# A state-space scan on one Trainium2 core: convolutions in column halves, relu moved to VectorE, small steps moved off it

## The reference, cut to what matters

```python
x = einsum('bld,ed->bel', ctx, in_proj_w)            # 512 channels
x = silu(causal_conv(x, conv_w, 4 taps) + conv_b)    # = u
dt_low, Bm, Cm = split(einsum('bdl,ed->bel', x, x_proj_w))
dt = softplus(einsum('brl,dr->bdl', dt_low, dt_proj_w) + dt_proj_b)
A  = -exp(A_log)                                     # 16 states a channel
# for each position l, channel d and state n:
#   state = state * exp(dt*A) + dt*u*B ;  y[d] = sum_n state*C
y = (y + D*u) * silu(layernorm(input x))
```

## Time and profile before

| | us |
|---|---|
| three runs | 1542.57, 1548.24, 1553.94; median 1548.24 |
| the profiled execution | 1534.55 |
| its span in the profile | 1532.7 |
| first scan to last scan | 45.1 to 451.5 |
| VectorE, ScalarE, TensorE, GpSimd busy over the span | 1098.2, 995.3, 1423.5, 639.0 |

### The profile page before, as it was taken

The page is one execution under the profiler, slowest core; times in us unless marked ns, Lnnn a source line. Parts: engine busy times, 40 slices in busy tenths (PEclk is TensorE's granted clock), DMA queues, the critical chain, the costliest instruction groups (busy, mean ns, idle before and its releaser), DMA issues. The chain is left out here.

```text
span 1532.7 us, 20749 instructions
## 1 busy us (share of the span) xinstructions
PE 1423.5 (93%) x6056; PEld 611.8 (40%) x6057; DVE 1098.2 (72%) x1603; ACT 995.3 (65%) x1538; POOL 639.0 (42%) x422
## 2 busy tenths in 40 slices
PE   6688988978988999999999899799999999999999
PEld 2344444434444444444444344233333333244444
DVE  7999999999995522222222488899999999548985
ACT  4999999999974112333332244588878787868764
POOL 0579689688976431075757555200000000410000
PEclk7799999999998999999999999799999999999999
DMA  6212314113206349778943656433233233430464
GB/s 200 65 50 85 94 56 124 41 56 111 76 1 215 116 138 181 186 207 275 322 130 98 215 175 166 119 83 76 76 93 79 74 79 94 147 110 14 93 145 119
DMA packets 181210, 183.45 MB, mean 120 GB/s; under 512 B 104611, under 2 KB 132643, under 8 KB 180371
## 3 DMA queue, kind: packets, MB, share of 16 engines
q1 hardware_dynamic: 114422, 128.02, 29.0%
q10 hardware_dynamic: 57776, 24.89, 6.8%
q0 software_dynamic: 8944, 29.70, 6.4%
HBM read 96.97 MB, written 54.92 MB: 99 GB/s over the span
## 5 line engine op out<-in xcount | busy, mean ns | idle before, releaser
L275 POOL TENSOR_TENSOR m_hs<-m_hs,m_C 128x1024 f32<-128x1024 f32 x128 | 305.2, 2403 | 61.5 <-DVE m_hs L496 60.5
L1929 DVE TENSOR_REDUCE a_mx<-a_s 128x2 f32<-128x1024 f32 x256 | 303.3, 1218 | 32.7 <-PE a_s L2049 29.2
L496 DVE TENSOR_TENSOR_SCAN m_hs<-m_dA,m_d 128x512 f32<-128x512 f32 x256 | 294.8, 1201 | 12.3 <-PE m_d L650 11.1
L650 PE MATMUL m_d<-ident_sb,m_dBuT 128*128 128x128 f32 x1024 | 159.1, 288 | 25.1 <-DVE m_hs L496 16.7
L650 PEld LDWEIGHTS m_d<-ident_sb,m_dBuT 128*128 128x128 f32 x1024 | 116.4, 145 | 149.7 <-DVE m_hs L496 70.5
L383 ACT ACTIVATE m_dA<-m_dt,m_negA 128x512 f32<-128x512 f32 x256 | 167.8, 711 | 6.8 <-DMA m_dt<-m_dt 6.1
L1367 PE MATMUL e_gu<-e_w,e_xgT 128*128 x376 | 169.2, 593 | 0.0
L1762 POOL TENSOR_TENSOR x_sb<-x_sb,bo_sb 128x512 f32<-128x512 f32 x16 | 19.7, 1292 | 341.7 <-DVE a_m L1945 341.7
L2049 PE MATMUL a_s<-ring_sb 96*128 96x512 bf16 x512 | 151.1, 387 | 7.2 <-DVE a_mx L1929 5.1
L361 ACT ACTIVATE m_dBuT<-m_dtuT,m_BT 128x512 f32<-128x512 f32 x235 | 154.1, 711 | 0.4 <-PE m_d L650 0.3
L665 PE MATMUL m_y<-m_hs,m_fold 128*64 128x512 f32 x512 | 142.6, 637 | 0.5 <-POOL m_hs L275 0.5
(11 more groups left out here) (342 smaller groups left out, 2346.3 us busy)
## 6 DMA issues: line engine op xcount, KB each, us to landing
e_w<-in_ex_gu SPq DMA_DIRECT2D x16, 1024.0 KB, 7.3
ring_sb<-qk_dram SPq DMA_DIRECT2D x64, 192.0 KB, 3.1
xg_dram<-zeros_sb SPq DMA_DIRECT2D x47, 256.0 KB, 3.1
yg_dram<-attn_sb ACTq DMA_DIRECT2D x47, 256.0 KB, 3.8
m_C<-c_dram SPq DMA_DIRECT2D x64, 128.0 KB, 2.9
m_dt<-m_dt SPq DMA_DIRECT2D x64, 128.0 KB, 2.4
e_w<-in_ex_dn SPq DMA_DIRECT2D x16, 512.0 KB, 8.9
ring_sb<-qk_dram SPq DMA_DIRECT2D x64, 128.0 KB, 3.2
```

The lines of the kernel that those rows point to most:

```text
L275: pool.tensor_tensor(hs[:, J % RH], hs[:, J % RH], C2[:, N % RC].unsqueeze(1).broadcast_to([P, 2, L]), ALU.mult).then_inc(s_hc, 1)
L496: dve.tensor_tensor_scan(hs[:, J % RH, h], dA[:, j % RA], pd[j % RD][:], 0.0, ALU.mult, ALU.add)\
L650: last = pe.transpose(pd[j % RD][:, t * P:(t + 1) * P], dBuT[:, N % 2, t, g], ident[:])
L1929: dve.tensor_reduce(mx[:, r % 2, h * TB + 2 * c:h * TB + 2 * c + 2], psc[c][:], AX.X, ALU.max)\
```

## The change

1. `convolve`: each of the four steps is done in two halves of 256 columns. A half waits for its own half's step before, so there are two chains. 8 instructions a tile (`TAPS`), 128 in place of 64.
2. For the batches 1 to 3, the relu of dt leaves ScalarE's `logs` and becomes `relu` on VectorE: for tile 0 between the two scans of slot 12, for the others behind the scans of slots 14, 17 and 20 and ahead of `log1p` and L486. ScalarE waits for it before |z|.
3. Layer norm columns: EPS becomes the bias of ScalarE's root; the negated mean and its product with 1/std are made by GpSimd behind its products of slots 2 and 3 of batch 0.
4. Slot 127: GpSimd multiplies only the first half by C, VectorE the second, right behind the last scan. The order after it changes: VectorE gate sums 0 to 2, add 0, gate sum 3, adds 1 and 2, small steps, add 3; TensorE turns tiles 0 and 1, then takes the sums of slot 127, then turns tiles 2 and 3.

```diff
 # GpSimd
+                if J == LAST - 1:
+                    pool.wait_ge(s_scan, 2 * J + 1)
+                    pool.tensor_tensor(hs[:, J % RH, 0], hs[:, J % RH, 0], C2[:, N % RC], ALU.mult).then_inc(s_hc, 1)
+                    continue
...
+                if J == 2:
+                    pool.wait_ge(s_ln, LN_VAR)
+                    pool.tensor_scalar(nmr[:], mv[:, :, 0], -1.0, None, ALU.mult).then_inc(s_nm0, 1)
+                if J == 3:
+                    pool.wait_ge(s_ln, LN_RSTD)
+                    pool.wait_ge(s_nm0, 1)
+                    pool.tensor_tensor(nmr[:], nmr[:], rstd[:], ALU.mult).then_inc(s_nm, 1)
 # ScalarE, gates
-                    act.wait_ge(s_ln, LN_READY)
+                    act.wait_ge(s_nm, 1)
 # ScalarE, logs
                 if p >= 1:
-                    act.wait_ge(s_d2[et], 64 * p)
-                    act.wait_ge(s_dtu, m - E4 + 1)
+                    act.wait_ge(s_rel, m + 1)
                 z = bank(p, et)
                 act.activation(ee[:, et % 2], z[:], ACT.Abs, bias=dt_b[:, et:et + 1]).then_inc(s_abs, 1)
-                act.activation(dt[:, et], z[:], ACT.Relu, bias=dt_b[:, et:et + 1]).then_inc(s_rel, 1)
+                if p == 0:
+                    act.activation(dt[:, et], z[:], ACT.Relu, bias=dt_b[:, et:et + 1]).then_inc(s_rel, 1)
 # ScalarE, slot 3 of batch 0
-                        act.activation(rstd[:], rstd[:], ACT.Sqrt).then_inc(s_sd, 1)
+                        act.wait_ge(s_eps, 1)
+                        act.activation(rstd[:], mv[:, :, 1], ACT.Sqrt, bias=lead[:, 2, 0:1]).then_inc(s_sd, 1)
 # VectorE, convolve
-                dve.tensor_scalar(conv[:, et], z[:], conv_w[:, et, 3:4], None, ALU.mult).then_inc(s_cv, 1)
+                for lo in (0, L // 2):
+                    dve.tensor_scalar(conv[:, et, lo:lo + L // 2], z[:, lo:lo + L // 2], conv_w[:, et, 3:4], None,
+                                      ALU.mult).then_inc(s_cv, 1)
                 for k in range(1, 4):
-                    dve.wait_ge(s_cv, 4 * m + k)
-                    dve.scalar_tensor_tensor(conv[:, et, k:L], z[:, 0:L - k], conv_w[:, et, 3 - k:4 - k],
-                                             conv[:, et, k:L], ALU.mult, ALU.add).then_inc(s_cv, 1)
+                    for i, lo, hi in ((0, k, L // 2), (1, L // 2, L)):
+                        dve.wait_ge(s_cv, TAPS * m + 2 * k - 1 + i)
+                        dve.scalar_tensor_tensor(conv[:, et, lo:hi], z[:, lo - k:hi - k], conv_w[:, et, 3 - k:4 - k],
+                                                 conv[:, et, lo:hi], ALU.mult, ALU.add).then_inc(s_cv, 1)
+
+            def relu(p, et):
+                m = E4 * p + et
+                dve.wait_ge(s_dtp, m + 1)
+                dve.wait_ge(s_d2[et], 64 * p)
+                dve.wait_ge(s_dtu, m - E4 + 1)
+                dve.tensor_scalar(dt[:, et], bank(p, et)[:], dt_b[:, et:et + 1], 0.0, ALU.add, ALU.max).then_inc(s_rel, 1)
 # VectorE, layer norm: L524 (+EPS) and L530 (negated mean times 1/std) removed
 # VectorE, loop over slots
                 scan(J, 0)
+                if p < B and s == 12:
+                    relu(p, 0)
                 scan(J, 1)
+                if J == LAST - 1:
+                    N = J // E4
+                    dve.wait_ge(s_c[N % RC], 32 * (N // RC + 1))
+                    dve.wait_ge(s_scan, 2 * LAST)
+                    dve.tensor_tensor(hs[:, J % RH, 1], hs[:, J % RH, 1], C2[:, N % RC], ALU.mult).then_inc(s_hl, 1)
...
+                if p < B and s in (14, 17, 20):
+                    relu(p, (s - 11) // 3)
                 if p < B and s in (13, 15, 18, 21):
                     log1p(p, (s - 12) // 3)
```

More of the change, by code:

```diff
@@ L28 @@
 EPS = 1e-5
-LN_VAR = 2 * NT + 1
-LN_RSTD = 2 * NT + 2
-LN_READY = 2 * NT + 3
+LN_VAR = 2 * NT
+LN_RSTD = 2 * NT + 1
 def mamba(nc, x_sb, ident, identb, tg, a, c_dram, xg_dram, zeros, s_zero, lead):
@@ L43, in mamba @@
     AHEAD = RA // 2 - 1
+    TAPS = 8
     EARLY = NT - 2
@@ L110, in mamba @@
         s_sd = sem("ln_std")
+        s_nm0 = sem("ln_mean_negated")
+        s_nm = sem("ln_columns_ready")
         s_negA0 = sem("expA")
@@ L138, in mamba @@
         s_hc = sem("output_terms")
+        s_hl = sem("last_output_terms")
         s_y = sem("summed")
@@ L292, in silu @@
                 for et in parts:
-                    act.wait_ge(s_cv, 4 * (E4 * p + et + 1))
+                    act.wait_ge(s_cv, TAPS * (E4 * p + et + 1))
                     if p >= 1:
@@ L522, in variances_last @@
                     dve.bn_aggr(mv[:, t], stats[:, t]).then_inc(s_ln, 1)
-                dve.wait_ge(s_ln, 2 * NT)
-                dve.tensor_scalar(rstd[:], mv[:, :, 1], EPS, None, ALU.add).then_inc(s_ln, 1)
             def ln_columns():
@@ L528, in ln_columns @@
                 dve.reciprocal(rstd[:], rstd[:]).then_inc(s_ln, 1)
-                dve.wait_ge(s_ln, LN_RSTD)
-                dve.scalar_tensor_tensor(nmr[:], mv[:, :, 0], -1.0, rstd[:], ALU.mult, ALU.mult).then_inc(s_ln, 1)
             dve.wait_ge(s_wa, 16 * 5)
@@ L563, in _ @@
                 gate_sum(B - 1, et)
-            for et in range(E4 - 1):
-                add(B - 1, et)
+            add(B - 1, 0)
+            gate_sum(B - 1, E4 - 1)
+            add(B - 1, 1)
+            add(B - 1, 2)
             dve.wait_ge(s_lead, 2 * TB + 2)
@@ L569, in _ @@
             dve.tensor_tensor(lead[:, 0], lead[:, 0], lead[:, 1], ALU.mult).then_inc(s_lead, 1)
-            gate_sum(B - 1, E4 - 1)
             add(B - 1, E4 - 1)
@@ L582, in project @@
                 if p >= 1 and et >= 1:
-                    pe.wait_ge(s_cv, 4 * (E4 * p + et))
+                    pe.wait_ge(s_cv, TAPS * (E4 * p + et))
                 if p >= 3 and et == 0:
@@ L596, in project_u @@
                     if et == 0 and p >= 1:
-                        pe.wait_ge(s_cv, 4 * E4 * (p + 1))
+                        pe.wait_ge(s_cv, TAPS * E4 * (p + 1))
                     last = pe.matmul((py[0] if p == 0 else pm)[0:RX, :], w_xp[:, et], u[:, et], start=(et == 0),
@@ L613, in dt_product @@
                 if p == 0:
-                    pe.wait_ge(s_cv, 4 * (et + 1))
+                    pe.wait_ge(s_cv, TAPS * (et + 1))
                 elif et == 0:
@@ L663, in sums @@
                 pe.wait_ge(s_hc, J + 1)
+                if J == LAST - 1:
+                    pe.wait_ge(s_hl, 1)
                 for h in range(2):
@@ L723, in _ @@
             pe.wait_ge(s_scan, 2 * LAST)
-            for et in range(E4 - 1):
+            for et in range(2):
                 turn(B - 1, et)
             sums(LAST - 1)
-            turn(B - 1, E4 - 1)
+            for et in range(2, E4):
+                turn(B - 1, et)
 NE = 16
```

## The result

| | before | after |
|---|---|---|
| median of the runs, us | 1550.32 (6 runs, 1542.57 to 1556.23) | 1570.23 (6 runs, 1559.05 to 1577.48) |
| profiled execution, span | 1532.7 | 1568.4 |
| first scan to last scan | 405.2 | 430.9 |
| last scan's end to the stage's last add | 6.8 | 7.7 |
| the stage's last add ends at | 458.3 | 485.2 |

The ratio is 1.0138, with a 95% interval of 1.0099 to 1.0177: the change makes the kernel 21 us slower (15 to 27). Forecast was +12.3, in a range that holds the result. The scan stage alone is 26.9 us longer in these two profiles, and 22.7 us in a second pair (e10 and e11, 456.7 and 479.4). The other 8.9 us of the span lie in later stages, which the change doesn't touch and whose length varied from 1074 to 1094 us over the profiles of this study; nothing is concluded from them.

The account below looks back on a forecast made before the run. The prediction took VectorE's own instructions as the bound. Convolutions +3.0, layer norm -2.8, relus +11.3 and the end +0.8 gave +12.3 us, 1560.5 us from 1548.24, range 1541 to 1577.

Parts of the forecast that it names:

- rival 3: Convolutions: half steps don't overlap, each costs 0.52 us, 16 convolutions +18 us, total +27.7, 1576 us; chance 0.16.
- within 1%: Whole kernel: the time changes by no more than about 1% (15 us) either way; chance 0.75.
- three signs of being wrong: Scan stage: L486 stays at 0.46 us, TensorE's scan waits become long lower-clock pieces, or scans begin waiting for decays.
- Rival 2: Scan stage: ScalarE is the bound, relu and layer norm savings are gained, stalls aren't paid: 1538 us; chance 0.10.
- Convolutions: 16 convolutions on VectorE: eight half steps at 0.40 us, 3.20 against 3.01 us, +0.19 each, +3.0 us in all.
- Layer norm: Batch 0: VectorE without L524 gains 1.7 us, without L530 half of 2.2: together -2.8 us (-3.9 to -1.7).
- the gates still waiting about 1.4 us: Layer norm: ScalarE's gates get their columns from GpSimd at about the same moment as before, still waiting about 1.4 us.
- Relu, slot 12: Relu between two scans falls into their waits for TensorE: about +0.1 us a batch, no delay of ScalarE.
- Relu, slot 14: Relu puts L486 behind the start of GpSimd's product, so L486 waits for its end: +2.37 us a batch.
- Relu, slot 15: L475 now meets GpSimd's long product and takes 2.38 us instead of 1.14: +1.2 us a batch.
- Relu, slots 17 and 20: +0.66 us each, offset by VectorE's waits for the logarithm going away: about +0.1 us in sum a batch.
- The end: Slot 127: VectorE's half product waits for GpSimd's, its queue shifts 1.1 us, an idle 0.75 may go: +0.8 us.

Follow-up runs that it names:

- e10: The kernel before, profiled once more, unchanged: 403.8 us from first to last scan.
- e11: The changed kernel, profiled once more, unchanged: 425.2 us from first to last scan.
- e1: The changed kernel with the relus of batches 1 to 3 back on ScalarE: 402.7 us from first to last scan, ratio 1.0016 to the kernel before.
- e7: The kernel before with the layer norm part alone: 407.0 us from first to last scan, ratio 0.9987.
- e4: The changed kernel with TensorE's products to dt for tiles 2 and 3 one slot earlier: 417.1 us from first to last scan.
- e6: The changed kernel with L486 ahead of slot 14's relu and tiles 2 and 3's dt products one slot earlier: 410.6 us first to last scan, ratio 1.0043.
- e9: The changed kernel with every relu between a slot's two scans, tiles 1 to 3's logs and corrections one slot later: 411.1 us first to last scan, ratio 1.0022.
- e3: The changed kernel with L486 issued ahead of the relu in slot 14: 416.6 us from first to last scan.
- e5: The kernel before, relu left on ScalarE, with unused VectorE work of like length at the relu's four places: 419.1 us from first to last scan.
- e8: The kernel before with the halved convolutions alone: 412.1 us from first to last scan.

## Why the prediction was right, and which steps of it were not

The sign, the stalls of slots 14 and 15 and the end were forecast with their mechanism and their size. That the result lies in the range is in part luck: the forecast of +12.3 us had its own span of 1550 to 1570 us, at whose upper end the measured time lies, and the top of the wider range, 1577, was worked out for rival 3, which is out. The likeliest call, within 1%, was missed (1.4%). Batch 1, forecast to be 4 us longer, was longer by 10.4 and 7.2. Of the three signs of being wrong one came: TensorE's lower clock, which rose from 58 and 65 us up to the last scan in the two profiles of the kernel before to 82 and 75 in those of the changed one, though the scans' own waits for TensorE stayed at 9.4 us (9.7 before).

- **What bounds.** VectorE's instructions set the pace and ScalarE doesn't, though both were full: e1 puts the relus back on ScalarE and is faster. Rival 2 is out.
- **Convolutions.** Forecast 3.20 us each; the changed kernel shows 3.10, from 52.50 to 55.60, and 5.95 against 5.83 for a slot that holds one. Half steps last 0.47 to 0.48 us, where 0.50 was forecast, and follow each other at 0.39 us in the mean.
```profile
52.50 0.84 DVE L479 TENSOR_SCALAR m_conv<-m_misc,m_conv_w 128x256 f32<-128x256 f32 x2
53.26 2.42 DVE L484 SCALAR_TENSOR_TENSOR m_conv<-m_misc,m_conv_w,m_conv 128x255 f32<-128x255 f32 x6
55.60 2.32 DVE L521 TENSOR_TENSOR_SCAN m_hs<-m_dA,m_d 128x512 f32<-128x512 f32 x2
```
  So +0.12 and not +0.19 each, +1.9 us for 16. Rival 3 is out: by it a slot would have grown by 1.1 us and not 0.12. The Trainium skill's page "VectorE: DVE Perf Modes", section "The DRAIN you can't avoid", says that a semaphore after each instruction costs nothing extra; this case's trace differs, with 0.77 us from start to start with a wait and 0.67 without. No run has the half steps with a wait for the one just ahead, so what they would cost isn't shown.
- **Layer norm.** -2.8 was forecast. By slots 0 to 8 of batch 0, without what the halves add, the second pair of profiles shows -2.2, the first -0.7 and e7 -0.2. VectorE did get the 1.7 and the 2.2 us (slot 4 starts 3.7 us earlier). The step that failed is "the gates still waiting about 1.4 us": they no longer wait and start at 67.83 us, not at 69.38. But ScalarE got no more than these 1.5 us, and in slot 7 VectorE stands before ScalarE's inputs: TensorE, which turns them, idles 2.70 us, and the first scan of slot 8 waits 2.50 us. The timelines of VectorE and of TensorE:
```profile
83.16 1.22 DVE L521 TENSOR_TENSOR_SCAN m_hs<-m_dA,m_d 128x512 f32<-128x512 f32 x1 [2.50 <-PE m_d L681]
```
```profile
82.42 0.66 PE L681 MATMUL m_d<-ident_sb,m_dBuT 128*128 128x128 f32 x4 [2.70 <-ACT m_dBuT L375]
```
  In all eight profiles with this part slot 8 starts 37.8 to 38.3 us behind the first scan, against 39.6 and 40.0 in the two of the kernel before. What follows differs. In the changed kernel's first profile, in e4 and in e7 TensorE's clock is at 1.2 GHz for 3.4 us from about 83.2 us on, slot 8 takes 4.53 us for 2.89, and the gain is gone; in e6 and e9 the clock falls near 82 us and slot 8 takes 3.8 us; in e1, e3 and e11 it stays full, slot 8 takes 2.89 us, and the gain stays. I had seen that ScalarE was full and didn't ask by how much it led. In e7 the two sides are 3.9 us each.
- **Relu, slot 12.** Covered, as forecast: 2.88 us in batches 1 and 2 of both profiles against 2.76 to 2.93 before, and 3.12 and 3.36 us in batch 0 against 3.00.
- **Relu, slot 14.** +2.37 forecast, +2.33 measured. That L486 stands still behind GpSimd's product, and that the order decides it, is shown by e3 (0.46 us with one swap) and e5 (2.21 us with other work of the same length). This is the rule of the Trainium skill's page "SBUF — State Buffer", section "Who interferes with whom"; the traces agree.
- **Relu, slot 15.** +1.2 forecast, +1.23 measured.
- **Relu, slots 17 and 20.** This is the term that was mis-sized: about +0.1 forecast for slots 17 to 21 together, +3.5 measured for slots 17 and 18, and between -0.4 and +3.1 for 20 and 21 in batch 1. The forecast held TensorE's product to be ready whenever VectorE came. L500's stall in slot 15 leaves TensorE idle, its clock goes down, and its queue puts a sum and a turn ahead of the product. The +3.5 are 1.65 us of waiting for it, 0.7 of relu and 1.7 more of L500 in slot 18, less the 0.54 us of waiting for the logarithm. e4 takes the product out of this and leaves exactly the forecast balance. With slots 14 and 15 the relus cost 25 us in the first pair of profiles and 21 in the second, above the forecast's bound of +17. The lower clock stood in the prediction only as the upper bound, +2 a batch, and rival 3's chance; it was the likelier course: the relu of slot 17 waited in all six batches of the two profiles.
- **The end.** +0.8 forecast, +0.87 in both profiles, and in e1 too. GpSimd's half runs 476.70 to 477.97, and VectorE's (L571) holds the queue until then; the timelines of VectorE and of GpSimd:
```profile
477.59 0.93 DVE L571 TENSOR_TENSOR m_hs<-m_hs,m_C 128x512 f32<-128x512 f32 x1
...
482.21 0.69 DVE L529 TENSOR_TENSOR m_ty<-m_y,m_gate 128x512 f32<-128x512 f32 x1 [0.58 <-PE m_y L698]
...
484.42 0.74 DVE L534 SCALAR_TENSOR_TENSOR x_sb<-m_misc,tg_sb,x_sb 128x512 f32<-128x512 f32 x1
```
```profile
476.70 1.27 POOL L279 TENSOR_TENSOR m_hs<-m_hs,m_C 128x512 f32<-128x512 f32 x1
```
- **The sum by what was measured**, second pair of profiles, first to last scan: slots 14 and 15 3 x 3.56 = 10.7, slots 17 to 21 4.1 + 3.2 + 3.2 = 10.4, the halves 12 x 0.12 = 1.4, layer norm -2.2: 20.3 of the 21.4 us. The rest is small pieces all over the stage. The size was off by the 10.4, for which 0.3 had been forecast; the sign was right, and the call "within 1%" was missed by the same amount.

What stays open: whether the halves by themselves make stretches at the lower clock likelier (e8), and why one execution has them in other slots than the next.

## What to carry to other kernels

Before VectorE work is added ahead of an instruction with two SBUF operands, or a copy-like one from SBUF to SBUF, look up when GpSimd's next instruction is released: here 0.7 us of work cost 3.6, since it let a 2.4 us instruction go first, twice. Then follow the engine that becomes idle: TensorE's stall came back as sums, turns and a product at half clock, for which the moved relu waited. And an engine that is full isn't thereby the bound: taking the relus off ScalarE paid nothing that a run shows, while of VectorE's gain in layer norm at most as much was left as ScalarE could follow.

## What the runs showed that I had not expected

- TensorE idled 2.2 us of the 3 us before 230.0; its clock was then granted at 1.2 GHz for 3.4 us, and with the product's place in the queue that was worth the 3.5 us of slots 17 and 18, which e4 takes back.
- The execution to execution difference of one kernel lies in such stretches: 3.03 or 4.72 us for slot 20 of batch 1 and 4.27 or 6.07 for slot 21, with the slots 14 to 18 ahead of them equal to 0.14 us.
- On GpSimd the two small steps with 16 columns take 0.25 and 0.22 us where VectorE's took 1.75 and 2.29 behind GpSimd's products:
```profile
60.45 0.25 POOL L286 TENSOR_SCALAR m_nmr<-m_mv 128x16 f32<-128x16 f32 x1
...
67.30 0.22 POOL L290 TENSOR_TENSOR m_nmr<-m_nmr,m_rstd 128x16 f32<-128x16 f32 x1
```
